# First attention of a fused four-layer kernel: feature distance and rounding as tensor operations, gate products read by whole bank, output bias added to x by GpSimd

## What is computed

```
emb = box_relational_embedding(boxes)            # 128 x 128 pairs of boxes, 16 features
g   = relu(einsum('bnmd,hd->bhnm', emb, Wg) + bg)
a   = einsum('bhqd,bhkd->bhqk', q, k) / sqrt(64)
mn  = softmax(log(clip(g, 1e-6)) + a)            # that is: max(g, 1e-6) * exp(a), normalised
out = einsum('bhqk,bhkd->bqhd', mn, v) @ Wo.T + bo
x   = x + tanh(g_xattn[0]) * out
```

## Time and profile before

| | |
|---|---|
| median of 3 runs | 1238.87 us (1237.45 to 1240.89) |
| profiled execution | 1237.56 us, of which span 1235.7 us |
| busy, share of the span | PE 81%, PE weight loads 65%, DVE 71%, ACT 55%, POOL 58% |
| mean granted TensorE clock | 0.921 of full speed |

### The profile page before, as it was taken

The page is one execution under the profiler, slowest core; times in us unless marked ns, Lnnn a source line. Parts: engine busy times, 40 slices in busy tenths (PEclk is TensorE's granted clock), DMA queues, the critical chain, the costliest instruction groups (busy, mean ns, idle before and its releaser), DMA issues.

```text
span 1235.7 us, 33130 instructions
## 1 busy us (share of the span) xinstructions
PE 996.9 (81%) x12306; PEld 805.0 (65%) x12306; DVE 872.5 (71%) x2036; ACT 684.3 (55%) x1338; POOL 711.1 (58%) x807
## 2 busy tenths in 40 slices
PE   0558999999999975678967389982999999999995
PEld 0436777777777754545633377761888888888884
DVE  4999998998888867468767778846555555555552
ACT  2447878787778863255345378743444444444442
POOL 2976788876775561035413578842556656566562
PEclk9869999999999987689989589975999999999998
DMA  9165766666676654400011000004352125721141
GB/s 284 41 140 106 129 136 136 135 112 127 136 145 121 120 112 123 181 1 1 1 39 31 1 2 20 19 32 167 104 138 63 26 64 153 246 62 28 30 132 14
DMA packets 48999, 112.99 MB, mean 91 GB/s; under 512 B 6032, under 2 KB 28560, under 8 KB 48512
## 3 DMA queue, kind: packets, MB, share of 16 engines
q0 software_dynamic: 14144, 35.48, 19.9%
q1 hardware_dynamic: 32400, 74.02, 18.0%
q10 hardware_dynamic: 2352, 2.10, 0.5%
HBM read 209.20 MB, written 34.50 MB: 197 GB/s over the span
## 4 chain that ended last, share of the span: by engine, by line
PE 54%; DVE 22%; POOL 10%; issue 6%; ACT 4%; DMA 2%; DVEq 1%; ACTq 0%; SPq 0%; POOLq 0%
PE bank L2080 12%; PE bank L2094 8%; POOL PT L531 5%; PE bank L1755 5%; PE bank L1655 2%; PE bank L1712 2%; PE bank L1716 2%; PE bank L1735 2%; DVE h L1030 2%; PE bank L1694 2%; DVE nmx L1144 2%; DVE PT L888 2%; PE bank L1989 2%; PE bank L1644 2%; PE bank L1912 2%
## 5 line engine op out<-in xcount | busy, mean ns | idle before, releaser
L1589 ACT ACTIVATE yg<-bank,bms 128x128 f32<-128x128 f32 x312 | 104.7, 361 | 130.8 <-PE bank L2080 128.4
L1265 DVE TENSOR_TENSOR hm<-hf,hm 128x256 f16<-128x256 f32 x156 | 66.5, 426 | 152.7 <-ACT hm L1596 152.7
L2080 PE MATMUL bank<-xT,wm_even 128*128 128x128 f16 x1920 | 117.1, 221 | 13.6 <-DVE hf L1260 12.7
L674 POOL DMA_INDIRECT out_x<-ys,sidx x39 | 62.7, 1608 | 112.2 <-DVE ys L1279 112.2
L2080 PEld LDWEIGHTS bank<-xT,wm_even 128*128 128x128 f16 x1920 | 110.6, 99 | 19.0 <-DVE hf L1260 14.1
L2080 PE MATMUL bank<-xT,wm_odd 128*128 128x128 f16 x1824 | 109.7, 219 | 12.3 <-DVE hf L1260 12.3
L2080 PEld LDWEIGHTS bank<-xT,wm_odd 128*128 128x128 f16 x1824 | 103.5, 98 | 17.2 <-DVE hf L1260 14.1
L1596 ACT ACTIVATE hm<-hf 128x256 f16<-128x256 f32 x156 | 64.6, 414 | 85.6 <-DVE hf L1260 85.6
L531 POOL TENSOR_TENSOR PT<-PT 128x512 f16<-128x512 f32 x64 | 72.2, 1152 | 66.1 <-ACT PT L1387 66.1
L1260 DVE SCALAR_TENSOR_TENSOR hf<-bank,bms,yg 128x128 f32<-128x128 f32 x312 | 94.4, 344 | 7.2 <-ACT yg L1589 7.2
L587 POOL TENSOR_TENSOR h<-h 128x512 f16<-128x512 f32 x32 | 40.6, 1282 | 83.0 <-DVE h L1030 80.9
(11 more groups left out here) (307 smaller groups left out, 2773.1 us busy)
## 6 DMA issues: line engine op xcount, KB each, us to landing
wm_even<-expert_weights SPq DMA_DIRECT2D x60, 1024.0 KB
wm_odd<-expert_weights SPq DMA_DIRECT2D x57, 1024.0 KB
expert_weights<-in_wcat POOLq DMA_DIRECT2D x16, 768.0 KB, 6.9
wsp<-expert_weights SPq DMA_DIRECT2D x16, 768.0 KB, 4.4
wsp<-in_wcat POOLq DMA_DIRECT2D x16, 768.0 KB, 9.6
expert_weights<-wsp SPq DMA_DIRECT2D x16, 768.0 KB, 3.5
expert_tokens<-xs SPq DMA_DIRECT2D x4, 520.0 KB, 4.9
X<-in_x ACTq DMA_DIRECT2D x1, 2048.0 KB, 15.3
```

What stands on the lines that cost most here:

```text
L674: nc.gpsimd.indirect_dma_start(out=a["out"], out_offset=bass.IndirectOffsetOnAxis(ap=sidx[:, t:t + 1], axis=0), in_=ys[:, t % 2, :], in_of ...
L1265: v.tensor_tensor(hm16[:, par, 1, c - 1:c + 1, :], hf[:, q % 2, :, :], hm16[:, par, 0, c - 1:c + 1, :], ALU.subtract).then_inc(m_hl, 1)
L1589: s.activation(yg[:, c % 4, :], bank[c % 4][:, 0:MT], ACT.Gelu, bias=bms[:, par, c:c + 1]).then_inc(m_g, 1)
L2080: ins = t.matmul(bank[c % 4][:, w * MT:(w + 1) * MT], wm16[par][:, wp, col:col + P], xT16[:, par, xp * KD + kk, :], start=(n == 0), stop=( ...
```

## The change

`feature_distance` becomes two instructions over all 1024 elements with broadcast operands instead of eight over 128, with a wait between them. The rounding takes its second constant from a broadcast column of the tile `cst` instead of an immediate. `probs` handles a whole bank in one instruction; for that TensorE writes the gate with the head outside and the group inside, so the columns of a matmul land in PSUM in pieces of 16 elements rather than in one row. The output bias is multiplied by tanh once (VectorE, ahead of iteration 0), GpSimd adds it to each tile of X in the new function `out_bias` after that tile's normalised copy was taken, and `residual` is one instruction that reads bank 7.

```
+            def out_bias(c):
+                if c == 0:
+                    gp.wait_ge(s_bo, 1)
+                gp.wait_ge(s_xn, c + 1)
+                nc.gpsimd.tensor_tensor(X[:, c, :], X[:, c, :], bo[:, :], ALU.add).then_inc(s_ba, 1)
...
                     split_ctx(b + 2, par)
+                for c in range(0 if b == 0 else b + 1, min(b + 2, B)):
+                    out_bias(c)
                 if has_s:
...
             def feature_distance(n, par):
-
-                for j in range(NJ):
-                    ins = v.tensor_scalar(fu[:, par, j * N:(j + 1) * N], cm[:, bass.ds(n * N, N)],
-                                          cn[:, bass.ds(n * NJ + j, 1)], rw[:, bass.ds(n * NJ + j, 1)],
-                                          ALU.subtract, ALU.mult)
-                ins.then_inc(s_fd, 1)
+                f = fu[:, par, :].rearrange("p (j n) -> p j n", j=NJ)
+                step(v.tensor_tensor(f, cm[:, n * N:(n + 1) * N].unsqueeze(1).to_broadcast([P, NJ, N]),
+                                     cn[:, n * NJ:(n + 1) * NJ].unsqueeze(2).to_broadcast([P, NJ, N]), ALU.subtract))
+                v.tensor_tensor(f, f, rw[:, n * NJ:(n + 1) * NJ].unsqueeze(2).to_broadcast([P, NJ, N]), ALU.mult).then_inc(s_fd, 1)
...
-                v.tensor_scalar(fk, fu[:, par, :], ROUND, ROUND, ALU.add, ALU.subtract).then_inc(s_fv, 1)
+                v.scalar_tensor_tensor(fk, fu[:, par, :], ROUND, cst[:, 6:7].to_broadcast([P, NJ * N]), ALU.add, ALU.subtract).then_inc(s_fv, 1)
...
             def residual(c):
                 dv.wait_ge(s_op, c + 1)
-                v.tensor_tensor(otmp[:, :], bank[7][:, 0:D], bo[:, :], ALU.add).then_inc(s_opt, 1)
-                dv.wait_ge(s_opt, c + 1)
-                xb = X[:, bass.ds(c, 1), :]
-                v.scalar_tensor_tensor(xb, otmp[:, :].unsqueeze(1), tg[:, 0:1], xb, ALU.mult, ALU.add).then_inc(s_xu, 1)
+                dv.wait_ge(s_ba, c + 1)
+                v.scalar_tensor_tensor(X[:, c, :], bank[7][:, 0:D], tg[:, 0:1], X[:, c, :], ALU.mult, ALU.add).then_inc(s_xu, 1)
...
-                    for jj in range(2):
-                        j = 2 * g + jj
-                        v.scalar_tensor_tensor(PT[:, :, j * NN:(j + 1) * NN],
-                                               bank[2 + g][:, jj * 256:(jj + 1) * 256].rearrange("p (h n) -> p h n", h=H), 1e-6 * GSC,
-                                               EX[:, :, j * NN:(j + 1) * NN], ALU.max, ALU.mult).then_inc(s_pm, 1)
+                    cols = slice(2 * g * NN, (2 * g + 2) * NN)
+                    v.scalar_tensor_tensor(PT[:, :, cols], bank[2 + g][:, :].rearrange("p (h n) -> p h n", h=H), 1e-6 * GSC,
+                                           EX[:, :, cols], ALU.max, ALU.mult).then_inc(s_pm, 1)
...
             dv.wait_ge(s_tg, 1)
+            v.tensor_scalar(bo[:, :], bo[:, :], tg[:, 0:1], None, ALU.mult).then_inc(s_bo, 1)
...
-                bk = bank[2 + g]
+                bk = bank[2 + g][:, :].rearrange("p (h j n) -> p j h n", j=2, h=H)
...
-                    t.matmul(bk[:, :], Rm16[:, bass.ds(b, 1), rp, :], Lw16[:, grp, lp, 2 * g:2 * g + 2, :], start=(n == 0), stop=(n == 2))
+                    t.matmul(bk, Rm16[:, bass.ds(b, 1), rp, :], Lw16[:, grp, lp, 2 * g:2 * g + 2, :], start=(n == 0), stop=(n == 2))
...
-                        ins = t.matmul(bk[:, jj * 256:(jj + 1) * 256], F16s[:, par, fp, j * N:(j + 1) * N], We16[:, wp, :], start=False,
+                        ins = t.matmul(bk[:, jj, :, :], F16s[:, par, fp, j * N:(j + 1) * N], We16[:, wp, :], start=False,
```

More of the change, by code:

```diff
@@ L136, in build @@
         warm = sb("warm", [P, 1], F32, att)
-        otmp = sb("otmp", [P, D], F32, att)
         pre = ExitStack()
@@ L287, in build @@
         s_ot, s_oc = sem("o_turned"), sem("o_turned_taken")
-        s_op, s_opt, s_xu, s_bs, s_bn = sem("proj_full"), sem("proj_taken"), sem("x_updated"), sem("bn_stats_done"), sem("stats_ready")
-        s_out = sem("stored")
+        s_op, s_bo, s_ba, s_xu, s_bs, s_bn = sem("proj_full"), sem("out_bias_scaled"), sem("out_bias_added"), sem("x_updated"), sem("bn_stats_done"), sem("stats_ready")
         f_ld, f_m, f_lp, f_low, f_tp, f_hi, f_lo = (sem("ffn_" + n) for n in (
@@ L1359, in exps @@
                     if g == 0 and not first:
-                        ac.wait_ge(s_pm, 8 * b)
+                        ac.wait_ge(s_pm, 4 * b)
                     s.activation(EX[:, HS * g:HS * g + HS, :], bank[g % 2][:, :].rearrange("p (h n) -> p h n", h=HS), ACT.Exp,
@@ L1383, in probs_high @@
                     if g == 0:
-                        ac.wait_ge(s_pm, 8 * c + 8)
+                        ac.wait_ge(s_pm, 4 * c + 4)
                         if not first:
@@ L1637, in project_qk @@
                     elif not first:
-                        pe.wait_ge(s_pm, 8 * b + 2 * r - 14)
+                        pe.wait_ge(s_pm, 4 * b + r - 7)
                     for c in range(HS):
@@ L1708, in gate @@
                 if not first:
-                    pe.wait_ge(s_pm, 8 * b - 8 + 2 * g + 2)
-                bk = bank[2 + g]
+                    pe.wait_ge(s_pm, 4 * b - 4 + g + 1)
+                bk = bank[2 + g][:, :].rearrange("p (h j n) -> p j h n", j=2, h=H)
                 for n, (lp, rp) in enumerate(PAIRS):
-                    t.matmul(bk[:, :], Rm16[:, bass.ds(b, 1), rp, :], Lw16[:, grp, lp, 2 * g:2 * g + 2, :], start=(n == 0), stop=(n == 2))
+                    t.matmul(bk, Rm16[:, bass.ds(b, 1), rp, :], Lw16[:, grp, lp, 2 * g:2 * g + 2, :], start=(n == 0), stop=(n == 2))
                 for jj in range(2):
@@ L1728, in pv @@
                         if not first:
-                            pe.wait_ge(s_opt, c)
+                            pe.wait_ge(s_xu, c)
                     else:
@@ L1811, in _ @@
             pe.wait_ge(s_qe, 6 * B)
-            pe.wait_ge(s_opt, B)
+            pe.wait_ge(s_xu, B)
             t.matmul(bank[4][0:RANK, 0:D], lowr[:, FF:FF + RANK], lowr[:, FF + RANK:], start=True, stop=True).then_inc(f_mp, 1)
@@ L2155, in arrange @@
     cst = np.zeros((P, 8), np.float32)
+    cst[:, 6] = ROUND
     for p in range(P):
```

## The result

The changed kernel takes 1249.08 us (median of 7 runs, 1246.39 to 1252.78) where the kernel before takes 1238.61 beside it (7 runs, 1234.63 to 1243.58): a ratio of 1.0091, with a 95% interval of 1.0071 to 1.0111. It is slower by 0.9%. Predicted were 1227.5 us and a range of 1220 to 1241, so both miss. Its profiled execution took 1246.39 us with a span of 1244.6; the granted clock is that of before (0.922 for 0.921).

A forecast was written before the change was run, and what follows sets the result against it. VectorE was taken to bound the first regime and the stretch ahead of iteration 0, not the second regime. Gains 3.8 + 1.1 + 5.1 + 1.2 = 11.2 us gave 1227.5 us against the runs, range 1220 to 1241.

The forecast's parts named there:

- I take 1.6: Rounding on VectorE beside GpSimd: waits for one operation, taking 1.6 us for 4.63, gaining 3.0 us an iteration.
- the first regime: Six loops of 25.60 us from 125.18 to 278.81, all with `separable` on GpSimd; VectorE taken to be in the loop.
- The first rival: Rounding still waits out GpSimd's whole run and takes 6.0 us, +1.1 an iteration, total 1240.3 us; chance 18%.
- the 5.1 us ahead of iteration 0: Net gain from shorter distances, VectorE being the limit there: 7.0 us less slower roundings and the scaling of `bo`.
- Six loops: Loops of 25.60 us with `separable` fall by 0.64 each to the other limit, 24.96: 3.8 us gained.
- The loop of 26.10: Single loop between the two regimes, where L813 waited for a GpSimd operation; expected to fall to 24.96, gaining 1.1 us.
- the second rival: GpSimd or L818/L813 becomes the limit in the first regime, or L813 misses its slot each loop: 1232.4 to 1237; 10%.
- The second regime: Six loops of 24.96 us from 304.91 to 454.69, VectorE not limiting; predicted no gain, its savings becoming wait.
- Probs: `probs` on VectorE by whole bank, four instructions of twice the length for eight: some 0.27 us saved.
- Tail: Last iteration, VectorE limiting up to `probs`, and last residual ahead of the statistics: 1.2 us gained.
- GpSimd in the loops: First regime: new bias and hold-ups by VectorE add 4.1 us against slack of 4.0; costed at nothing.
- 12% given to the rival: Scattered PSUM write slows TensorE's gate matmuls, at half pace +67 us, 1295 with the gains; chance 12%.

The follow-up runs named there:

- The best kernel found: Kernel before with gate products by whole bank and GpSimd's per-iteration high-half DMA issue moved behind the context split: 1228.92 us, ratio 0.9940.

## Why the prediction was wrong

*The failed step on the path* is "I take 1.6: every two-operand row I have waited for one operation at most". The rounding took 5.83 in the first regime and 4.70 in the second. The first rival had the mechanism and the size in the loops: it gave 6.0, and +1.1 an iteration; measured are +1.21 for the rounding, -0.90 `residual`, +0.77 distance, -0.26 products, which is +0.82, the growth of the loops. Its total of 1240.3 was too low, since it kept the gain ahead of iteration 0. The row that misled was the 1.39 of the earlier trace rows: it shows a two-operand instruction in a run of GpSimd that no DMA issue precedes, and the rounding stands behind one. The sentence against it stood in the prediction itself, "all the slow cases start just as GpSimd's DMA issue ends", but it got 18% and the forecast 60%.

The prediction cited the Trainium skill, SBUF — State Buffer, section "Who interferes with whom", for a wait of one instruction. That the new form doesn't escape GpSimd was right; the length of the wait agrees with the rows that have no issue ahead (1.41, 1.50) and not with the closed runs (4.63 to 9.91 for an instruction of 1024 elements).

*The second failed step* is the 5.1 us ahead of iteration 0. The distances did shrink (L813 at 57.89 takes 1.53, and the row maximum that stood at 67.03 stands at 60.87). But "TensorE's idle of 7.71 shrinks by as much; behind it [...] follow" took VectorE for the only limit. The runs show two things in its place: q waits 4.36 us for GpSimd, whose list slipped by 3.9 us, and VectorE then meets closed runs that it had passed before because it came later, or, at the distances of iteration 0, because its own instruction was still at work as the issue ended (6.79 for 0.81 in the scaling; 1.22 and 6.38 for 4.10 in the distances of iteration 0). The size: -5.1 predicted, +5.0 measured, 10.1 us. Against the profiled execution, which the forecast put at 1226.4 and which took 1246.39, the 20.0 us are: 10.1 here, 8.7 in the six loops, 0.8 in the first loop, 1.1 in the loop that took over the missed slot, 2.3 less for the end of the stage, 1.6 behind it. That two-operand instructions of VectorE are what slows GpSimd is argued from where the q split starts: at 64.92 to 67.11 in all nine kernels with the new early distances and the split in its old place, at 60.86 to 63.05 in the eight with the old ones. Beside a distance of two operands a `separable` instruction of 0.62 took 1.59 and 1.62 (L490).

*Six loops, -3.8 predicted, +4.9 measured.* The limit of 24.96 was right: every kernel with the closed run opened reached it, or 25.1 where the gap behind the feature split was added as well.

*The loop of 26.10* fell to 24.97, as said, but the missed slot of 1.64 came back in a later loop (26.08), which the second rival had described; the two cancel.

*The second regime* kept 24.97: the rounding grew by 1.2 there and the distance by some 0.4, and what the residual saves, the 0.77 of cover and the shorter products took it. Outside the loop of 26.08 no idle stands ahead of `probs` any more. *Probs* -0.26 for -0.27, right. *Tail*: the last loop is 1.2 shorter, the size of that term, and from the last copy to the last residual another 2.3 went that no term had; 1.2 was too small. *GpSimd in the loops*: costed at nothing, and rightly so for its own slack, but the bias lengthened the closed run by 0.7, and VectorE paid; the prediction had that in its rival and not in its sum. *TensorE*: nothing, right, 12% given to the rival. There too the Trainium skill, PSUM — Partial Sum Buffer, section "Specifications (TRN2)", says that a non-contiguous pattern slows matmuls significantly; pieces of 64 bytes don't, by the 385 and 388 ns. Two sums of the rivals don't come out of their rows, and nothing hangs on them: the 5.2 us of gate matmuls an iteration stand in no row (the two lines together cover 5.7 us an iteration), and the second rival's 1.8 is 1.3, as its seventh loop was already 26.10.

What stays open: why the changed kernel with both kinds of issue moved is slower than with one, why one run of the seven stayed open, and how much of the wait ahead of iteration 0 could be had by a full rearrangement of GpSimd's list there. The best kernel found leaves the distances, the rounding and the bias as they were.

## What to carry to other kernels

When a VectorE instruction takes several times its own run, look at what GpSimd did just before it: if a DMA issue stands there with tensor work packed behind it, move the issue behind that work or open a gap, before rewriting the instruction, and see what the issue then stands in front of. Work that is made shorter changes when everything behind it arrives; read from the trace of GpSimd what it will arrive beside. And an instruction added to a run that another engine waits out costs that engine its length, however much slack its own engine has.

## What the hardware showed that was not expected

A DMA issue by GpSimd, followed at once by its tensor instructions, kept VectorE out to the end of the run in 110 of 117 cases, whatever the VectorE instruction: one operand (4.63, 6.79, 8.94, 9.91 us), two (5.16, 5.83, 6.38), or two small ones (6.65 for 1.28). Without the issue, beside the same instructions, it waited for one of them at most (1.41, 1.50). It got in behind an issue too where its own two-operand instruction was still at work as the issue ended (0.64 to 1.16). A wait of GpSimd for its own result in the run had nearly the same effect (1.80).

The price of opening the run is some 1.9 us on GpSimd: the v split takes 3.11 for 2.2 and the context split 1.65 for 0.7.

A matmul whose output lands in PSUM in pieces of 16 floats took 385 to 388 ns for 512 columns, the same as one that lands in a row.
